# Quad-head attention rebuilt on one pass of scores and transposed exponentials; masked-head copies moved four banks behind

## The reference

```python
x = x + attention(layernorm(x)) @ Wo + bo      # per batch of 256 tokens
```

## Time and profile before

| | us |
|---|---|
| runs, median of 3 (lowest to highest) | 1761.01 (1760.57 to 1762.17) |
| the profiled execution, its own time | 1761.7 |
| its span (first to last instruction) | 1760.0 |
| TensorE busy | 1415.8 (80%) |
| VectorE busy | 875.7 (50%) |
| ScalarE busy | 756.1 (43%) |
| GpSimd busy | 430.4 (24%) |
| layer 0's quad stage | 29.1 to 414.6 |
| layer 2's quad stage | 951.6 to 1161 |
| layer 3's masked stage | 1407 to 1637 |
| mean granted TensorE clock, share of full speed | 0.908 |

### The profile page before, as it was taken

One profiled execution on the slowest core, in us unless ns is written; L12 is line 12 of the kernel. 1 busy time (PEld: TensorE's weight loads), 2 busy tenths in 40 slices (PEclk: granted clock), 3 DMA queues, 4 the chain that ended last, 5 costly groups with the idle time before them and its releaser, 6 DMA issues. The chain is left out here.

```text
span 1760.0 us, 27583 instructions
## 1 busy us (share of the span) xinstructions
PE 1415.8 (80%) x10001; PEld 785.2 (45%) x10001; DVE 875.7 (50%) x2460; ACT 756.1 (43%) x1609; POOL 430.4 (24%) x513
## 2 busy tenths in 40 slices
PE   6899999997899999885997899976083577787585
PEld 4344444444544444463455344455062434444364
DVE  4555555542355555455213565447223657666433
ACT  3244443443177777451440133443020467776233
POOL 4533333310121110100001444201544042210134
PEclk9999999998999999895999999987586889999687
DMA  7900000000000000000003100000122000000022
GB/s 209 133 1 1 2 1 1 1 1 0 1 1 1 1 1 1 1 1 1 1 1 127 51 1 1 1 1 10 51 80 78 1 19 13 7 13 1 7 59 77
DMA packets 60255, 42.31 MB, mean 24 GB/s; under 512 B 13189, under 2 KB 54121, under 8 KB 60121
## 3 DMA queue, kind: packets, MB, share of 16 engines
q1 hardware_dynamic: 54752, 32.42, 7.7%
q0 software_dynamic: 3552, 7.33, 1.2%
q10 hardware_dynamic: 1816, 0.81, 0.2%
HBM read 25.88 MB, written 14.66 MB: 23 GB/s over the span
## 5 line engine op out<-in xcount | busy, mean ns | idle before, releaser
L885 ACT ACTIVATE L0a_probs<-L0a_psL 128x512 f32<-128x512 f32 x192 | 104.2, 594 | 202.0 <-PE L0a_psL L693 73.5
L1262 ACT ACTIVATE L3x_e<-L3x_e,L3x_neg_max 128x256 f32<-128x256 f32 x256 | 112.4, 499 | 55.8 <-DVE L3x_neg_max L1314 55.2
L949 DVE TENSOR_REDUCE L0a_mx_part<-L0a_psS 128x4 f32<-128x512 f32 x120 | 77.3, 686 | 105.6 <-PE L0a_psS L636 81.3
L1182 PE MATMUL L3x_psE<-ident,L3x_e 128*128 128x128 f32 x512 | 84.3, 297 | 38.6 <-ACT L3x_e L1262 25.1
L1314 DVE CUSTOM_DVE_ANT_0 L3x_e<-L3x_psS,L3x_mask_rows 128x256 f32<-128x256 f32 x256 | 93.5, 420 | 31.2 <-PE L3x_psS L1174 30.9
L538 POOL TENSOR_SCALAR L0a_km<-L0a_kT,quad_rows 128x256 f32<-128x256 f32 x64 | 58.4, 930 | 199.3 <-ACT L0a_kT L856 199.3
L628 PE MATMUL L0a_psS<-L0a_km,L0a_qT 32*128 32x512 f32 x360 | 101.4, 640 | 0.2 <-DVE L0a_mx_part L954 0.2
L885 ACT ACTIVATE L2a_probs<-L2a_psL 128x512 f32<-128x512 f32 x96 | 52.1, 595 | 107.3 <-PE L2a_psL L689 72.5
L1182 PEld LDWEIGHTS L3x_psE<-ident,L3x_e 128*128 128x128 f32 x512 | 58.6, 149 | 87.2 <-ACT L3x_e L1262 68.3
L662 PE MATMUL L0a_psL<-L0a_qm,L0a_kT 32*128 32x512 f32 x256 | 72.1, 637 | 21.8 <-DVE L0a_mx L949 20.3
L1516 PE MATMUL L1a_psL<-L1a_soft_near,neg_tri 128*128 128x512 f32 x128 | 67.9, 612 | 0.2 <-DVE L1a_soft_near L1723 0.2
(11 more groups left out here) (719 smaller groups left out, 3476.4 us busy)
## 6 DMA issues: line engine op xcount, KB each, us to landing
L2f_rows<-packed_rows SPq DMA_DIRECT2D x8, 325.0 KB
packed_rows<-zeros SPq DMA_DIRECT2D x1, 2560.0 KB, 32.4
experts_L_L<-in_L_ffn_w_dram SPq DMA_DIRECT2D x1, 2048.0 KB, 8.9
unpacked_rows<-zeros SPq DMA_DIRECT2D x1, 2048.0 KB, 22.5
scores_L_experts_L<-in_L_ffn_w_dram SPq DMA_DIRECT2D x1, 2048.0 KB, 8.0
L2f_back_rows<-unpacked_rows SPq DMA_DIRECT2D x16, 128.0 KB, 2.6
L3x_mask_rows<-in_mask_Bx1xSxS_ff_dram SPq DMA_DIRECT2D x8, 256.0 KB, 2.7
sorted_rows<-zeros SPq DMA_DIRECT2D x1, 1472.0 KB, 20.1
```

Source lines behind the costliest of these rows:

```text
L885: nc.scalar.activation(probs[:, half, a, k, :], psL[i % RING][:], ACT.Exp, scale=scale).then_inc(s_prob, 1)
L949: nc.vector.tensor_reduce(dst, psS[a][:].rearrange("p (j n) -> p j n", j=4), AX.X, ALU.max).then_inc(s_red, 1)
L1182: last = nc.tensor.transpose(psE[i % 2][:, c * P:(c + 1) * P], e[:, i % RING, c * P:(c + 1) * P], mem.ident[:])
L1262: last = nc.scalar.activation(at, at, ACT.Exp, bias=neg[:, i % RING, j:j + 1], scale=-1.0)
```

## The change

The form of `masked_heads` is given to `quad_heads`: scores are made once, the maximum comes off in SBUF, the exponentials are transposed by TensorE and copied. Two lists of `masked_heads` are also put in another order. `Hidden` goes, masks are now kept as rows (`causal_rows` is new, built in the prologue by a memset and two selects on GpSimd). In the quad form a batch has 12 banks in three groups; the first group holds the first 128 queries against the first 128 keys, four heads to a bank, so its reduction works in four pieces of 128, and the exponential's bias would be four columns: there GpSimd subtracts the maxima (`take_off_max`) and ScalarE takes one exponential of the whole bank. `divide` and `next_h` move from VectorE to GpSimd, `keep_h` and `keep_raw` from ScalarE to VectorE; `qm`, `mx`, `nm`, `psL` and `psN` go.

```diff
 quad_heads
-    KINDS = ((0, 0), (1, 0), (1, 1))
-    SLOTS, ITEMS, SLOT = 6, 12, 32
-    RING = 3
+    GROUPS, ITEMS, SLOT, RING = 3, 12, 32, 8
+        def place(i):
+            b, n = divmod(i, ITEMS)
+            g, r = divmod(n, 4)
+            return b, g, r
+        def pieces(i):
+            return 4 if place(i)[1] == 0 else 2
+        def kept_at(i):
+            _, g, r = place(i)
+            return probs[:, r, :, 0:P] if g == 0 else probs[:, r, 2 * g - 2:2 * g, P:3 * P]
 gpsimd
+                def take_off_max(i):
+                    pool.wait_ge(s_red, i + 1)
+                    at = e[:, i % RING, :].rearrange("p (j n) -> p j n", j=4)
+                    nc.gpsimd.tensor_tensor(at, at, neg[:, i % RING, :].unsqueeze(2).to_broadcast([P, 4, P]), ALU.subtract).then_inc(s_less, 1)
+                next_h(0)
+                next_h(1)
+                nc.gpsimd.memset(v[:], 0.0).then_inc(consts, 1)
+                pool.wait_ge(consts, 1)
+                for i in range(3):
...
+                for b in range(2):
+                    if rope:
+                        combine(b)
+                    variants(b)
+                    next_h(b + 2)
                 for b in range(NB):
+                    for r in range(4):
+                        take_off_max(ITEMS * b + r)
+                    if b + 2 < NB:
+                        if rope:
+                            combine(b + 2)
+                        variants(b + 2)
                     if biased:
+                        add_bias(b)
+                    if b > 0:
+                        divide(b - 1)
+                    if b + 4 < NB:
+                        next_h(b + 4)
+                divide(NB - 1)
 tensor
+                def score(group):
+                    b, g = divmod(group, GROUPS)
+                    if group >= 1:
+                        pe.wait_ge(s_red, 4 * group)
+                    if g == 0:
+                        pe.wait_ge(s_km, b + 1)
                     for r in range(4):
                         rows = slice(32 * r, 32 * r + 32)
+                        if g == 0:
+                            nc.tensor.matmul(psS[r][:], qT[rows, b % 3, 0:P], km[rows, b % 3, :, 0:P], start=True, stop=True).then_inc(s_score, 1)
+                        else:
+                            nc.tensor.matmul(psS[r][:], qT[rows, b % 3, P:S], km[rows, b % 3, 2 * g - 2:2 * g, :],
+                                             start=True, stop=True).then_inc(s_score, 1)
+                def turn_exp(i):
+                    pe.wait_ge(s_exp, i + 1)
+                    if i >= 2:
+                        wait_kept(pe, i - 2)
+                    for c in range(4):
+                        last = nc.tensor.transpose(psE[i % 2][:, c * P:(c + 1) * P], e[:, i % RING, c * P:(c + 1) * P], mem.ident[:])
+                    last.then_inc(s_et, 1)
                     if b == 1:
-                        first_scores(0)
+                        warm(6)
+                        score(0)
                     values(b)
                 turn(2)
                 for b in range(NB):
+                    for n in range(ITEMS):
+                        i = ITEMS * b + n
+                        g, r = divmod(n, 4)
+                        if r == 1 and i + 3 < LAST:
+                            score(i // 4 + 1)
+                        if n == 0 and b > 0:
+                            weigh(b - 1, 0)
+                            weigh(b - 1, 1)
+                        if n == 1 and b > 0:
+                            weigh(b - 1, 2)
+                        if n == 2 and b > 0:
+                            weigh(b - 1, 3)
+                        if n == 3 and b + 2 < NB:
+                            queries(b + 2)
+                        if n == 5 and b > 0:
+                            spread_sums(b - 1)
+                        if n == 5 and b + 2 < NB and rope:
+                            keys(b + 2)
+                        if n == 7 and b + 2 < NB:
+                            values(b + 2)
+                        if n == 10 and b > 0:
+                            project(b - 1)
+                        if n == 10 and b + 3 < NB:
+                            turn(b + 3)
+                        turn_exp(i)
 scalar
+                def exponent(i):
+                    b, g, r = place(i)
+                    if g == 0:
+                        act.wait_ge(s_less, 4 * b + r + 1)
+                        nc.scalar.activation(e[:, i % RING, :], e[:, i % RING, :], ACT.Exp, scale=-1.0).then_inc(s_exp, 1)
+                    else:
+                        act.wait_ge(s_red, i + 1)
+                        for j in range(2):
+                            at = e[:, i % RING, j * S:(j + 1) * S]
+                            last = nc.scalar.activation(at, at, ACT.Exp, bias=neg[:, i % RING, j:j + 1], scale=-1.0)
+                        last.then_inc(s_exp, 1)
+                for i in range(LAST):
+                    b, n = divmod(i, ITEMS)
+                    exponent(i)
+                    if i >= 2 and i % 2 == 0:
+                        keep(i - 2)
+                    if n == 3 and 2 <= b and b - 2 + B < NB:
+                        scale_rows(b - 2)
+                    if n == 5 and b + 2 < NB and not rope:
+                        keep_qk(b + 2)
+                    if n == 7 and b > 0:
+                        invert(b - 1)
 vector
+                dve.wait_ge(consts, 4)
+                def reduce(i):
+                    b, g, r = place(i)
+                    n = 512 // pieces(i)
+                    hidden = of(b).mask[:, 0, 0:P] if g == 0 else of(b).mask[:, 1, :]
...
+                    for j in range(pieces(i)):
+                        at = slice(j * n, (j + 1) * n)
+                        last = nc.vector.tensor_tensor_reduce(out=e[:, i % RING, at], in0=psS[r][:, at], in1=hidden, scale=-scale, scalar=MOST,
+                                                              op0=ALU.add, op1=ALU.min, accum_out=neg[:, i % RING, j:j + 1])
+                    last.then_inc(s_red, 1)
+                for i in range(LAST):
+                    b, n = divmod(i, ITEMS)
+                    reduce(i)
+                    if i % 2 == 1 and i >= 4:
+                        keep(i - 4)
+                    if n == 0 and b >= 2:
+                        settle_x(b - 2)
+                    if n == 2 and b + 2 < NB:
+                        keep_h(b + 2)
+                    if n == 6 and b > 0:
+                        keep_raw(b - 1)
+                    if n == 7 and b + 2 < NB and rope:
+                        rotate(b + 2)
+                    if n == 9 and b + 2 < NB and rope:
+                        rotate_keys(b + 2)
+                    if n == 11 and b + 2 < NB:
+                        keep_v(b + 2)
+                settle_x(NB - 2)
+                keep(LAST - 3)
+                keep(LAST - 1)
+                keep_raw(NB - 1)
 masked_heads, tensor
-                        if r == 2 and i + 2 < LAST:
+                        if r == 1 and i + 3 < LAST:
                             score(i // 4 + 1)
 masked_heads, scalar
-                    if n == 6 and b > 0:
+                    if n == 7 and b > 0:
                         invert(b - 1)
-                    if n == 9 and b + 2 < B:
+                    if n == 10 and b + 2 < B:
                         keep_h(b + 2)
 masked_heads, vector
-                    if n % 4 == 0 and i > 0:
-                        keep(i - 1)
-                    if n % 4 == 3:
-                        keep(i - 2)
-                    if n == 14 and b > 0:
-                        settle_x(b - 1)
+                    if i % 2 == 1 and i >= 4:
+                        keep(i - 4)
+                    if n == 0 and b >= 2:
+                        settle_x(b - 2)
+                settle_x(B - 2)
+                keep(LAST - 3)
                 keep(LAST - 1)
                 settle_x(B - 1)
```

439 lines of the change are left out of this document (111 added, 328 removed).

## The result

| | us |
|---|---|
| kernel after, median of 8 runs (lowest to highest) | 1753.8 (1748.1 to 1759.6) |
| kernel before, beside it, median of 8 runs | 1761.6 |
| ratio after/before | 0.9955, 95% interval 0.9934 to 0.9975 |
| profiled execution after, its own time (span) | 1758.4 (1756.4) |
| granted TensorE clock, before and after | 0.908, 0.877 |

The change makes the kernel faster by 0.45%, about a quarter of what was forecast. The direction held, the size did not. The profiled execution after is one of the slower of its eight, so its stages may be a few microseconds longer than usual. First the page of the kernel after: TensorE's busy line and its clock in 40 slices.

What follows compares the result with a forecast made beforehand. TensorE, 92% busy, was taken to bound the quad stages, and hand-overs layer 3. Layer 0 -31, layer 2 +11 and layer 3 -9 summed to -29 us against 1761.7: 1732 us, range 1703 to 1768.

Steps and rivals of the forecast that it cites:

- all three terms: Whole kernel, by stage: layer 0 31 us shorter, layer 2 11 us longer, layer 3 9 us shorter.
- Pieces 0.22 apart: First group's VectorE reductions: 128-wide pieces follow each other after 0.22 us, 0.88 a bank.
- Layer 2's loss: Layer 2's quad stage: GpSimd's key sum, variants and divide delay `project`, +2.7 us in batches 2 to 6; stage +11.
- the 1.25 us wait: Layer 3: VectorE's copies wait 1.25 us at a time for transposes; the new order was to remove this.
- The check of the hand count on the present layer 3: Layer 3's present groups counted, 5.65, 6.37 and 7.2 against rows of 6.13, 6.28 and 6.99: add 1%.
- the clock term: All three stages: 0.5 us a batch for clock dips, from layer 3's 26.1 mean against 25.6; without it 12 us lower.
- the layout by hand: Layer 0, one steady batch laid out step by step from its first score matmul: 19.2 us, 19.4 with 1%.
- GpSimd in time in layer 2: First rival: in layer 2 a late batch lets GpSimd catch up, and the clock costs half: 1713 us, chance 0.2.
- The second rival: New form goes at layer 3's present rate, 1.63 us a bank; layer 3 gains nothing: 1759 us, chance 0.14.
- The slower case: Third rival: VectorE's 128-wide pieces in group 0 cost as much as 256-wide ones, 0.345: 1775 us, chance 0.13.
- The estimate of 1754: VectorE's 128-column pieces at 0.29 us by the skill's fp32 formula: a batch 0.9 us longer, whole kernel 1754.
- Its own signs of being wrong: Pieces at 0.3 or more, TensorE waiting long for first four banks' exponentials, VectorE's copies waiting over 1 us for transposes.

Runs made afterwards that it cites:

- e2_fill: Kernel after plus ten dummy 512-column matmuls in TensorE's wait ahead of bank 11's transpose, most batches of both quad stages: 1733.5 us, 0.9843 of before.
- e6: Kernel after plus ten dummy 512-column matmuls in TensorE's wait ahead of a batch's last bank, layer 3's masked stage alone: 1751.2 us, 0.9937 of before.
- e5: Kernel after with VectorE's `settle_x` moved behind the copy that follows reduction 1, in both quad stages and layer 3: 1685.4 us, 0.9567 of before.
- e11: Kernel after without GpSimd's subtraction of maxima, ScalarE taking four 128-column exponentials with bias instead: 1749.8 us, 0.9921 of before.
- e12: Kernel after with layer 2's divide early, `settle_x` behind the copy, and four biased ScalarE exponentials replacing GpSimd's subtraction: 1666.8 us, 0.9450 of before.

## Why the prediction was right and wrong

**Right.** The direction, and the signs of all three terms. Pieces 0.22 apart (forecast 0.22). Layer 2's loss and its place: TensorE's projection waiting 2.51 us for GpSimd's `yT`, a first group of 11.18 where 10.9 was forecast, and 2.8 us more than with the divide early, against +2.7. TensorE's wait in layer 0's first group ends 5.9 us behind the scores (193.84 to 199.72), forecast 5.8. In layer 3 the 1.25 us wait went.

**Right by luck.** Layer 3's stage with its dips filled gives -13.0 (215.9 against 228.9), and the sum without the clock has -13. But before's 228.9 has its dips in it. Undisturbed batches go from 25.56 to 25.06 and not to 24.4, which is 2.5 in the five middle batches; 7.3 there are before's dips, and the rest is at the ends of the stage. The check of the hand count on the present layer 3 asked for "1%", but it was 0.5 short in one group and 0.1 to 0.2 long in two.

**The step that failed: the clock term, 0.5 us a batch.** It makes 15.5 us in all three stages (7.5, 4, 4; the prediction's "12 us lower" leaves layer 3 out). The fills measure what dips took from the profiled execution: 12.9, 10.2 and 6.2, together 29.3. The four dips that e2_fill left in layer 2 made its first groups 0.9 longer each, so some 4 us more (an estimate), 33 in all.

Two things made the term too small. First, it was misread in its own witness: 26.1 a batch in layer 3 is a mean over seven intervals of raw copies, and the last of them is 22.3, as nothing follows it. Six batches before it take 26.78 each, 25.56 without a dip: 1.2 a batch for dips and not 0.5. Carried over to the same 31 batches, 1.2 makes some 37 us. Second, the wait that lets the clock fall in the new form was in the layout by hand ("TensorE waits for copy -3 till 5.8", 2.6 us behind TensorE's last work), and nothing was charged for it but its own length. A dip behind it costs 1.54 in layer 0 and 1.63 in layer 3. That the dips of the new form come from these waits is shown: filled (e2, e6) or shortened (e5), they leave no dip in the batches of layer 0 and layer 3 behind the start. The Trainium skill (TensorE: Matmul & The Clock Gate, Part 1) ties the clock to what TensorE has just done; the fills agree, as 30 us of useless matmuls shortened layer 0's stage by 12.9. The prediction cited that rule for the removed work, and should have applied it to the added wait.

**Smaller misses.** Layer 0's clean batch is 19.70, not 19.4 (its first group 8.47 against 8.24), 4.5 us over 15; its first scores came at 53.7, not 52.6 (in the traces with this start they come from 51.5 to 54.5). `take_off_max` takes 1.04 and not 1.27, and e11 and e12 show that it lies beside the path. Layer 2 was entered as +11 where its own line gives 11.7. From there to the total: 13.8 us of clock (29.3 - 15.5), 5.6 in layer 0's batches and start, 6.1 in unchanged code, less 0.7 in layer 2 (e2_fill's +6.3 over before, its four dips in it, against +7 without the clock term), make 24.8; from the forecast -29 to the -3.6 between the two spans it is 25.4.

**Rivals.** "GpSimd in time in layer 2" did not occur (2.51 us of wait in the trace), and the clock cost twice the term, not half of it. The second rival's time, 1759, lies near the 1753.8 measured, but not by its mechanism: the groups are not at layer 3's old rate, and layer 3 did gain. The slower case fell with the 0.22. The estimate of 1754 from the Trainium skill (VectorE: DVE Perf Modes, "The TRN2 errata") meets the measured time by chance: the duration of one piece, 0.29, agrees with that formula, but the next piece starts after 0.22, so that no batch is longer by it. (The page gives the formula for an addition out of SBUF; a piece here is a fused reduction out of PSUM.)

**What was not seen.** The wait of 2.6 us could be shortened by moving one call behind another. The prediction had the chain in full, reduction 0, `settle_x`, reduction 1, copy -3, and took it as given. Its own signs of being wrong (pieces at 0.3, a wait for the first exponentials, VectorE's copies waiting over 1 us for transposes) all stayed away, while the time missed: none of them looked at the clock.

## What to carry to other kernels

When a change takes work off a full engine, lay out one batch of the new form and look for the longest single wait of TensorE: it costs its length and, if the clock dips behind it, here 1.5 us more each time. In a chain that frees a buffer for TensorE or feeds it, work that can wait (on VectorE the addition to x, on GpSimd the key sum and the variants) belongs behind the step that TensorE waits for; order inside the queues was worth 5% here, the whole change of form 0.45%. When a pace is read as a mean from first to last, look whether the last interval is like the others. A filler of useless matmuls is a cheap test of whether a wait costs clock, and a poorer cure than shortening the wait (0.9725 against 0.9461, both with the divide early).
